# Moving eight row sends of a routed stage from the end of self attention into the stage itself

## The reference

```
hidden = resid + (ctx @ o_w + o_b)
xt = layer_norm(hidden, ln2_w, ln2_b).reshape(T, D)
logits = xt @ router_w
top1 = argmax(softmax(logits)); top2 = argmax(logits without top1)
loc1 = cumsum(m1, axis=0) - 1.0
loc2 = cumsum(m2, axis=0) - 1.0 + m1.sum(axis=0, keepdims=True)
slot1, slot2 = loc1, loc2 where they are below C
xin = each expert's rows, in slot order
h = gelu(xin @ fc1_w + fc1_b); eout = (h @ fc2_w + fc2_b) * 0.8
moe_out = g1 * eout[top1, slot1] + g2 * eout[top2, slot2]
```

## Time and profile before

| what | us |
|---|---|
| median of three runs | 1374.43 |
| profiled execution | 1372.78 |
| its span | 1371.0 |
| TensorE matmuls busy | 1111.6 (81% of the span) |
| VectorE busy | 703.0 (51%) |
| ScalarE busy | 614.7 (45%) |
| GpSimd busy | 464.9 (34%) |

### The profile page before, as it was taken

One profiled execution on the slowest core, in us unless ns is written; L12 is line 12 of the kernel. 1 busy time (PEld: TensorE's weight loads), 2 busy tenths in 40 slices (PEclk: granted clock), 3 DMA queues, 4 the chain that ended last, 5 costly groups with the idle time before them and its releaser, 6 DMA issues. The chain is left out here.

```text
span 1371.0 us, 26647 instructions
## 1 busy us (share of the span) xinstructions
PE 1111.6 (81%) x8678; PEld 762.6 (56%) x8678; DVE 703.0 (51%) x3350; ACT 614.7 (45%) x1531; POOL 464.9 (34%) x693
## 2 busy tenths in 40 slices
PE   5997967299989999988898785889477999972783
PEld 3675845177864566664344574688362444442673
DVE  3564648233356777644444564011656788864002
ACT  3453544133358766624222242333362666641553
POOL 1674634433313655420000546344011000057243
PEclk9899989599999999999998796699785899985897
DMA  7499330213029990001541003465223122105433
GB/s 211 112 289 222 83 108 28 74 59 104 20 73 123 119 194 2 2 1 52 126 101 39 2 2 108 127 171 157 64 64 99 56 57 71 38 13 163 123 105 97
DMA packets 148022, 125.39 MB, mean 91 GB/s; under 512 B 14025, under 2 KB 124505, under 8 KB 147896
## 3 DMA queue, kind: packets, MB, share of 16 engines
q1 hardware_dynamic: 133016, 104.53, 32.8%
q0 software_dynamic: 7824, 15.47, 4.3%
q10 hardware_dynamic: 7056, 3.81, 1.0%
HBM read 88.91 MB, written 37.70 MB: 92 GB/s over the span
## 5 line engine op out<-in xcount | busy, mean ns | idle before, releaser
L325 POOL TENSOR_TENSOR L_Z<-L_Z,L_mx 128x512 f32<-128x512 f32 x84 | 88.6, 1056 | 104.7 <-DVE L_mx L675 104.7
L939 ACT ACTIVATE L_Z<-L_Z,L_nmx 128x154 f32<-128x154 f32 x256 | 105.2, 414 | 42.3 <-DVE L_nmx L989 42.2
L3294 DVE CUSTOM_DVE_ANT_0 L3s_masked<-L3s_psS,L3s_trilw 128x512 f32<-128x512 f32 (+3 forms) x256 | 109.7, 486 | 23.9 <-PE L3s_psS L3121 23.4
L3249 ACT ACTIVATE L3s_E<-L3s_psT 128x512 f32<-128x512 f32 (+1 forms) x192 | 87.7, 530 | 49.2 <-PE L3s_psT L3134 49.0
L808 POOL TENSOR_TENSOR L_Z<-L_Z,L_rin 128x488 f32<-128x488 f32 x64 | 64.0, 1000 | 111.4 <-DVE L_rin L997 111.4
L675 DVE CUSTOM_DVE_ANT_0 L_Z<-L_psS,L_Z 128x154 f32<-128x154 f32 x256 | 63.5, 314 | 60.9 <-PE L_psS L380 48.3
L850 PE MATMUL L_psS<-L1k_G,L_xnT 128*128 128x462 f32 x192 | 82.4, 525 | 3.0 <-DVE L_nmx L989 1.6
L989 DVE CUSTOM_DVE_ANT_0 L_Z<-L_psS,L_mask 128x154 f32<-128x154 f32 x256 | 67.9, 314 | 11.5 <-PE L_psS L850 10.3
L556 ACT ACTIVATE L_E<-L_psT 128x512 f32<-128x512 f32 x84 | 46.3, 596 | 56.9 <-PE L_psT L393 56.9
L1007 DVE COPY L_PT<-L_psT 122x512 f32<-122x512 f32 x64 | 43.7, 683 | 40.1 <-PE L_psT L860 39.3
L2338 DVE TENSOR_TENSOR L0f_h<-L0f_h,L0f_psB 128x384 f32<-128x384 f32 (+1 forms) x64 | 31.2, 487 | 63.1 <-PE L0f_psB L2300 59.3
(11 more groups left out here) (588 smaller groups left out, 2916.2 us busy)
## 6 DMA issues: line engine op xcount, KB each, us to landing
L_Z<-in_fside_Bx16xSxS SPq DMA_DIRECT2D x16, 1232.0 KB, 9.0
L2f_w<-in_L_ffn_W SPq DMA_DIRECT2D x39, 256.0 KB, 2.9
slotsL<-empty SPq DMA_DIRECT2D x1, 8320.5 KB, 75.3
L1m_cb<-comb_rows SPq DMA_DIRECT2D x8, 1024.0 KB, 10.0
L3f_w<-in_L_ffn_fc_w SPq DMA_DIRECT2D x32, 256.0 KB, 4.1
L0f_w<-in_L_ffn_W SPq DMA_DIRECT2D x24, 256.0 KB, 4.1
L3s_QS<-q_parts SPq DMA_DIRECT2D x144, 32.0 KB
L3s_KS<-k_parts SPq DMA_DIRECT2D x48, 96.0 KB
```

The costliest lines, as they stand in the source:

```text
L325: nc.gpsimd.tensor_tensor(Z[:, t % NZ, h, 0:KM_], Z[:, t % NZ, h, 0:KM_], top.broadcast_to([P, HG, KM_]), ALU.subtract).then_inc(z_ready, 1)
L939: last = nc.scalar.activation(Z[:, t % 2, h], Z[:, t % 2, h], ACT.Exp, scale=-1.0, bias=nmx[:, t % 2, h:h + 1], accum_out=sums[:, t % 2, h ...
L3249: nc.scalar.activation(E[:, g.par, h, EO[group[0]]:EO[group[0]] + wd], psT[:, k, 0:wd], ACT.Exp).then_inc(t_free, 1)
L3294: last = nc.vector.tensor_tensor_reduce(masked[:, k, at:at + wd], psS[:, k, at:at + wd], trilw[:, S - wd:S], 1.0, LOW, ALU.add, ALU.max, m ...
```

## The change

In the tail of self attention POOL no longer waits for the table to be wiped and for batch 0's rows, and no longer sends batch 0. `Last.SENT` goes from 1 to 0, so the loop at the start of the routed stage sends batches 0 to 3. Batches 0 and 1 are still routed and placed in the tail, and the three copies of rows stay there.

```diff
@@ -1899,7 +1899,7 @@
 class Last:
-    EARLY, ROUTED, SENT = 3, 2, 1
+    EARLY, ROUTED, SENT = 3, 2, 0
@@ -3095,11 +3095,6 @@
             route.root(pool, own, 2)
             route.second_copies(pool, 1)
-            pool.wait_ge(m.wiped, 64)
-            pool.wait_ge(route.slots_ready, 1)
-            pool.wait_ge(route.pay_done, 1)
-            last.seconds(pool, 0)
-            last.firsts(pool, 0)
             route.second_copies(pool, 2)
```

## The result

The changed kernel took 1382.41 us, the median of 17 runs (1375.62 to 1386.68), beside 1376.49 us (1370.90 to 1380.84) for 17 runs of the kernel before. The ratio is 1.0038, 95% interval 1.0027 to 1.0049: slower by 5.2 us, 3.7 to 6.7. The forecast was 5.6 us slower and 1379.5 us. The difference is under the 1% that is treated as no change for this kernel, but its interval excludes zero.

A forecast was written before the change was run, and what follows sets the result against it. POOL's last send was taken as the bound in this stretch, not TensorE. Eight more sends, 10.2 us, less a barrier 4.65 us earlier, gave +5.6 us; the sum reached 1380.0 us, 1379.5 was predicted, range 1373.5 to 1386.5.

The forecast's parts named there:

- barrier earlier: End of self attention: without early sends VectorE's drain, not POOL's, closes the stage, a gain of 4.65 us.
- eight more sends: Start of the routed stage: eight sends ahead of the 24, at 1.28 us each, add 10.2 us to the path.
- behind the last send: Expert loop and collection: the time after the last send stays as long as before, 101.1 us.
- The sends leave the tail: Tail of self attention: POOL's drain ends before 1227.3, VectorE's closes the stage at 1231.83; gain 4.65 us.
- the three waits: POOL's waits in the tail: said to cost nothing, as slots, rows and wiped table were ready long before.
- The sends enter the stage: Behind the barrier: first send 0.9 us after it, eight more cost 10.2 us, and POOL never waits.
- The long stall: Send beside line 1992: the 17th behind the barrier is again held up by 1.98 us, change 0.
- The first send: First early send's extra 0.24 us beside line 1493: its return behind the barrier bounded by 0 and 0.24, taken as 0.
- A: Starts of the loop's turns: TensorE's clock at the upper level saves up to 7.2 us, 1372.3, likelier 1376; chance 0.13.
- C: Expert loop: longer idling keeps TensorE at 1.2 GHz two units longer, +13.9 us, 1388 us; chance 0.07.
- Rival B: End of self attention: the barrier does not open earlier, so 4.65 us are not gained, 1384.1 us; chance 0.11.
- D: Tail sends: the change doesn't do what it says and the sends stay in effect hidden, 1374 us; chance 0.01.

The follow-up runs named there:

- e1: The changed kernel without batch 0's eight sends at all (result incomplete); 1368.28 us, ratio 0.9974 to the kernel before.
- e2: The kernel before with only batch 0's four second-choice sends left in the tail, its four first choices behind the barrier; 1373.99 us, ratio 1.0011.
- e5: The kernel before with line 1992's whole residual moved behind the routing shares and the landing of all sends; 1370.65 us, ratio 0.9979.
- e4: The changed kernel with line 1992's residual cut into sixteen instructions of 128 x 128; 1378.03 us, ratio 1.0033 to the kernel before.
- e8: The kernel before with line 1992's residual cut into sixteen instructions; one run, 1372.03 us.
- e3: The kernel before with sixteen sends in the tail, batches 0 and 1, instead of eight; 1383.69 us, ratio 1.0083.

## Why the prediction was right, step by step

| term | predicted | measured, from T |
|---|---|---|
| barrier earlier | 4.65 | 4.7 (20.4 to 15.7); e1: 4.5 at the last send |
| from barrier to first send | 0.9 | 0.9 |
| eight more sends | 10.2 | 10.2 (e1 to after) |
| the stalled send | 1.98, the 17th again | 1.99 (2.96), the 17th |
| end of the last send | +5.6 | +5.65 (53.8 to 59.5) |
| behind the last send | 101.1 | 101.0 |
| total | 1379.5, +5.6 | 1382.4; ratio gives +5.2 (3.7 to 6.7) |

*The sends leave the tail.* Right in its sum: POOL's drain was the last because of its sends. It ended 1.7 us behind the last early send before, 1.5 in e2, and at the end of the copy where there was none. The 0 to 0.35 us that the copy's new place might have added to the tail did not show: VectorE's drain ended at T + 15.6 (1236.2 + 0.3), and at T + 15.7 before (1231.8). One reading was wrong: the three waits did cost POOL time. The slots of batch 0 were not ready long before, but 0.85 us ahead of the first early send, and POOL had stood idle for 3.20 us by then. The sum does not feel it, since VectorE sets the barrier once the sends are gone; the number of sends that are free does.

*The sends enter the stage.* Right, and POOL waited neither for slots nor for a landing (2.1 to 5.3 us). The time at which POOL reaches batch 3 left out the 1.98 us of the stalled send ahead of it, so its slots came 13.7 us ahead (1256.82 against 1270.51) and not 11.6; nothing hangs on it.

*The long stall.* Right in size and place. Of the rule of the Trainium skill (SBUF — State Buffer, section SBUF: two separate sides) the trace had shown the part for one long instruction. The page has a condition that the prediction left out: two inputs in SBUF count only against a GpSimd instruction that reads SBUF. A send takes its offsets from `slot_to`, which lies there; no run here separates this. e5 shows that line 1992's instruction is the cause. e4 and e8 show that a row of short ones is neither free nor a full lock.

*The first send.* Its 0.24 us was bounded by 0 and 0.24; it took 1.08 us, 0.1 over the others.

*Rivals A and C.* The granted clock, TensorE only, of the changed kernel and then of the one before (columns as in the earlier trace rows). The first two lines of each are the first turn of the loop, the last is the second turn:

```profile
1284.00:1292.00 8.00, 6.34 (x16) 0.50 0.37 98
1292.00:1312.00 20.00, 19.37 (x123) 0.98 0.50 143
1327.00:1362.00 35.00, 32.33 (x200) 0.95 0.10 31
```

```profile
1273.50:1281.50 8.00, 6.26 (x17) 0.52 0.38 98
1281.50:1301.50 20.00, 19.25 (x128) 1.00 0.53 147
1322.00:1352.00 30.00, 27.43 (x186) 1.00 0.03 7
```

In the first turn, after 29.05 us of idling, the engine worked some eight microseconds at 1.2 GHz and then at 2.4, as after 18.86, so C did not happen. In the second turn a part of A did. Before, 1315 to 1322 at 0.52 means some 6.7 us at 1.2 GHz, ahead of the stretch in the line above; in the changed kernel 0.95 over 35 us means some 3.5 us, and 1320 to 1327 was at 0.99. So the work after which the clock came back was not the same every time, as the prediction had taken it to be. (In both kernels the second turn's first matmuls of line 2297 still ran at 2.4 GHz; the clock fell 1.5 to 2 us behind the first of them.) The gain was small: counted from the last send's end, the last matmul ended at 79.9 us instead of 80.4 and POOL's last send of results at 84.5 instead of 84.9, and the collection behind it took as much longer, 16.5 us instead of 16.1. *Rival B* fell with e1. *D* did not happen: the sends moved.

The level was off by 2.9 us: three runs of before with a median of 1374.43 stood 2.1 under what 17 showed, and I had taken 1379.5 rather than the sum's 1380.0. The first is the baseline's scatter, the second my choice; neither is a term of the change.

## What to carry to other kernels

Here work put ahead of the barrier was free only up to the second-last arrival, and could not begin before its own inputs were there. Read the drains at the join and the start of the first piece of work, and count between them: some four of eight sends fitted, the rest cost the same on either side, and without any the engine stood idle. Moving more across than fits delays every engine's start behind the barrier, which cost 10.7 us in e3. Where one engine's queue is the path, look for the single entry that lasts longer than its kind; moving line 1992 out of its way gained 2.0 us in the trace. And compare traces from the last untouched landmark, since here the end of the untouched 1216 us lay anywhere from 1209.6 to 1220.9 us in ten traces, twice what the change was worth.

## What the runs showed of the hardware that I had not expected

At this join POOL's drain lasted beyond the end of its last indirect DMA by 1.5 to 1.9 us (e2: 1.5; before: 1.7; e3: 1244.6 against 1242.7), though without such DMAs it ended with the last instruction to 0.1 us. A copy issued behind the sends added nothing to it: it was there in e2 and before, and not in e3. The figure belongs to this join: behind the scatters of results, lines 2382 and 2543, at three other joins of the kernel before, it was 4.7 (1359.55 against 1354.87), 5.1 and 5.9 us. What sets it was not tested.

Sixteen VectorE instructions of 128 x 128 back to back took 4.29 us against 2.35 in one, let two sends through at 0.97 and 0.99 us and held the next one to 2.32 us, twice at the same place. What decides which send is held was not settled.
